# A fused linear-attention and FP4 feed-forward kernel: SyncE's queue reordered, four cast buffers, attention read from four banks at once

## The reference, cut to what matters

```
xn  = layernorm(x)
# branch s: linear attention, then an MLP
a   = rmsnorm(xn);  q, k, v = a @ qkv_w.T          # 16 heads of 64
q, k = exp(-0.5*q*q), exp(-0.5*k*k)                # phi
kv  = k^T v per head, over the whole sequence of 2048 rows (16 tiles)
out = (q @ kv) / (q . sum(k) + 1e-6);  x1 = xn + gamma*(out @ proj_w.T + b)
s   = x1 + gamma*(gelu(rmsnorm(x1) @ conv1_w.T + b1) @ conv2_w.T + b2)
# branch g: feed-forward whose weights and inputs go through blockwise FP4
fq(z): per block of 16: scale = max|z|/6; round z/scale to the FP4 grid; times scale
h   = silu(fq(xn) @ fq(w_gate).T) * (fq(xn) @ fq(w_up).T)
g   = silu(fq(h) @ fq(w_down).T)
out = x + s*g
```

## Time and profile before

| | |
|---|---|
| three runs | 1999.74, 2073.59 and 1997.06 us; median 1999.74 |
| the profiled execution | 1997.77 us; spans of the cores 1979.4 to 1996.2 us |
| the core shown (core 1) | span 1996.2 us, mean granted TensorE clock 0.977 |
| stretch 50 to 484.6 us (stages 2 to 5) | 434.6 us, PE busy 363.1 |
| stretch 484.6 to 1020 us (stage 6) | 535.4 us, PE busy 516.4 |
| stretch 1020 us to the end (stage 7) | 976.2 us, PE busy 962.4 |

### The profile page before, as it was taken

One profiled execution on the slowest core, in us unless ns is written; L12 is line 12 of the kernel. 1 busy time (PEld: TensorE's weight loads), 2 busy tenths in 40 slices (PEclk: granted clock), 3 DMA queues, 4 the chain that ended last, 5 costly groups with the idle time before them and its releaser, 6 DMA issues.

```text
span 1996.2 us, 27757 instructions; the slowest of 8 cores (1979.4 to 1996.2 us)
## 1 busy us (share of the span) xinstructions
PE 1875.5 (94%) x9142; PEld 879.4 (44%) x9142; DVE 1636.2 (82%) x2019; ACT 785.3 (39%) x991; POOL 395.5 (20%) x356
## 2 busy tenths in 40 slices
PE   6988697878999999999999999999999999999997
PEld 3434343333444444444444444444444444444443
DVE  4788878867688688797734999999999999999986
ACT  4676576664433433544521222222222222222221
POOL 3245545534423422422500000000000000000000
PEclk9999898989999999999999999999999999999998
DMA  9788778884455465465599433444334333433322
GB/s 301 199 238 233 226 210 212 229 225 127 115 159 161 109 174 161 101 189 149 127 197 191 126 103 88 95 102 103 94 86 105 103 93 86 105 99 92 88 83 66
DMA packets 367262, 287.07 MB, mean 144 GB/s; under 512 B 299024, under 2 KB 308240, under 8 KB 366096
## 3 DMA queue, kind: packets, MB, share of 16 engines
q1 hardware_dynamic: 367120, 285.29, 55.3%
HBM read 153.63 MB, written 59.24 MB: 107 GB/s over the span
## 4 chain that ended last, share of the span: by engine, by line
PE 71%; DVE 8%; issue 7%; DMA 6%; ACT 3%; POOL 3%; SPq 2%; DVEq 0%; ACTq 0%; POOLq 0%
PE PS L1081 30%; PE PS L1126 15%; PE PS L900 10%; PE PS L883 8%; PE PS L840 5%; DMA xf<-w_gate 2%; DMA wst<-c1T 2%; PE PS L646 1%; DVE q_am L222 1%; DVE atz L817 1%; DVE ob L256 1%; PE PS L588 1%; DVE xf L231 1%; DMA xf<-w_up 1%; DMA phi_h<-pq 1%
## 5 line engine op out<-in xcount | busy, mean ns | idle before, releaser
L240 ACT ACTIVATE gam<-xf 128x1024 bf16<-128x1024 f32 (+1 forms) x196 | 198.1, 1011 | 505.1 <-DVE xf L231 494.5
L1081 PE MATMUL PS<-wg,xqT 128*128 128x512 bf16 (+1 forms) x1536 | 319.9, 361 | 1.7 <-DVE so L910 1.7
L1081 PE MATMUL PS<-wu,xqT 128*128 128x512 bf16 (+1 forms) x1536 | 319.9, 361 | 0.0
L222 DVE TENSOR_REDUCE q_am<-xf 128x64 f32<-128x1024 f32 (+1 forms) x196 | 227.6, 1161 | 74.5 <-DMA xf<-w_up 29.5
L250 DVE SCALAR_TENSOR_TENSOR xf<-gam,xf 128x1024 f32<-128x1024 bf16 (+1 forms) x196 | 233.9, 1193 | 30.0 <-ACT gam L240 29.7
L256 DVE SCALAR_TENSOR_TENSOR ob<-gam,q_sc 128x1024 bf16<-128x1024 bf16 (+1 forms) x196 | 243.0, 1240 | 3.3 <-DVE gam L253 2.8
L231 DVE SCALAR_TENSOR_TENSOR xf<-xf,q_rc 128x1024 f32<-128x1024 f32 (+1 forms) x196 | 238.0, 1214 | 1.9
L253 DVE SCALAR_TENSOR_TENSOR gam<-gam,xf 128x1024 bf16<-128x1024 bf16 (+1 forms) x196 | 235.6, 1202 | 2.1
L883 PE MATMUL PS<-xn2T,c1T_s 128*128 128x512 bf16 x1024 | 234.8, 384 | 2.4 <-DVE kvbd L566 2.4
L1126 PE MATMUL PS<-wdA,hqT 128*128 128x512 bf16 x1024 | 227.8, 380 | 0.4 <-DMA hqT<-ob 0.4
L900 PE MATMUL PS<-c2T_s,hdd 128*128 128x512 bf16 x1024 | 222.3, 379 | 0.0
(11 more groups left out here) (90 smaller groups left out, 1852.8 us busy)
## 6 DMA issues: line engine op xcount, KB each, us to landing
xx<-x SPq DMA_DIRECT2D x32, 512.0 KB, 4.5
xf<-x SPq DMA_DIRECT2D x32, 512.0 KB, 4.2
xr<-x SPq DMA_DIRECT2D x32, 512.0 KB, 4.6
out<-xr SPq DMA_DIRECT2D x31, 512.0 KB, 3.9
xa<-x SPq DMA_DIRECT2D x30, 512.0 KB, 6.0
stg<-qkvT SPq DMA_DIRECT2D x24, 512.0 KB, 13.2
xf<-w_gate SPq DMA_DIRECT2D x22, 512.0 KB, 6.3
xf<-w_up SPq DMA_DIRECT2D x22, 512.0 KB, 5.9
```

The lines of the kernel that those rows point to most:

```text
L222: S.add("v", lambda v: v.tensor_reduce(am, blk(y), AX, op.max, apply_absolute_value=True), waits=[src_ev, opt("q_nq%d" % (k - 3))], ev="q_ ...
L240: S.add("sc", lambda s: s.activation(gam[k % 2][:, 0:W], xf[k % 3][:, 0:W], AF.Abs, scale=BIG), waits=["q_y%d" % k, opt("q_out%d" % (k - 2 ...
L1081: S.add("pe", lambda pe, wts=wts, bi=bi, j=j, b0=b0, ic=ic: pe.matmul(bank(b0 + j, GB[bi][1]), xqT[t % 3][:, ic, :], wts[bi][:, ic, :], st ...
```

## The change

- **SP's order.** The phi(q) stores, the `xn1T` transposes and the `xa` loads that are asked for during one k, v or q group are put into SP's list at the head of the next (`later`, `held`). The store of a finished quantisation task goes behind the next task's load (`unsent`, `send`). Cast loads are asked for after the third group of a tile and not the second.
- **Cast buffers.** `wst` has four buffers for the first 28 pieces and two for the last 12; up to four are loaded ahead.
- **phi(q) buffers.** The last eight q groups have seven buffers (`pqx` and `pq`). `turn(31)` moves from the end of tile 27 behind the second of the 13 q groups.
- **Zeroing.** `zero_acc(1)` moves from tile 16 to the end of tile 17's groups, one tile later.
- **Attention.** From tile 4 on it lies in banks 0 to 3, two pairs of heads in each, and one DVE instruction each makes the denominators and `atz` instead of three. conv1 takes banks 4 to 7, conv2 banks 0 to 3.
- **xn2.** The ACT instruction that writes it is put one group later than the one that takes the squares (`proj_xn2`).

```diff
             [WK + 63552, WK + 64576, WK + 73792])]
-        wst = [at("wst%d" % i, [P, D], F32, WK + 65600 + 4096 * i) for i in range(2)]
+        wst = [at("wst%d" % i, [P, D], F32, o) for i, o in enumerate(
+            [WK + 65600, WK + 69696, W3 + 24576, W3 + 28672])]
+        pqx = [at("pqx%d" % i, [P, 512], BF16, WK + 24576 + 1024 * i) for i in range(4)]
...
                 if n == 1:
+                    send()
...
+        unsent = []
+        def send():
+            while unsent:
+                unsent.pop(0)()
...
-            def post(k):
+            def store(k):
...
                 S.ev[tk["done"]] = S.ev["q_st%d" % k]
+            def post(k):
+                unsent.append(lambda: store(k))
...
                 prev = cur
+            send()
...
                   waits=["mrs%d" % t, "x%d" % t, opt("xn1T%d" % (t - 2))], ev="xn1_%d" % t)
-            S.add("sy", lambda s: s.dma_start_transpose(out=xn1T[:, c, :, :], in_=xn1_of(t)[:]),
-                  waits=["xn1_%d" % t, opt("kv%d_3" % (t - 8)), opt("q%d_7" % (t // 4 - 2))],
-                  inc="XT%d" % (t % 4), ev="xn1T%d" % t)
+            later.append(lambda: S.add(
+                "sy", lambda s: s.dma_start_transpose(out=xn1T[:, c, :, :], in_=xn1_of(t)[:]),
+                waits=["xn1_%d" % t, opt("kv%d_3" % (t - 8)), opt("q%d_7" % (t // 4 - 2))],
+                inc="XT%d" % (t % 4), ev="xn1T%d" % t))
...
+        NW4 = 28
+        def wbuf(n):
+            return n % 4 if n < NW4 else n % 2
...
+            before = [m for m in range(n) if wbuf(m) == b]
...
-            S.add("sy", lambda s: s.dma_start(out=wst[n % 2][:],
+            S.add("sy", lambda s: s.dma_start(out=wst[b][:],
...
-                  waits=[opt("wc%d" % (n - 2))], inc="WS%d" % (n % 2), ev="wl%d" % n)
+                  waits=["wc%d" % before[-1] if before else "kvm3"], inc="WS%d" % b,
+                  ev="wl%d" % n)
...
                 dst = projT[:, ic, :] if kind == "p" else c2T[:, ic, :]
-                S.add("gp", lambda p: p.tensor_tensor(dst, wst[n % 2][:], gm[:], op.mult),
-                      waits=["wl%d" % n, "gm", "kvm3"], ev="wc%d" % n)
+                w = ["wc%d" % (NW4 - 1), "wc%d" % (NW4 - 2)] if kind == "2" and ic >= 12 else []
+                S.add("gp", lambda p: p.tensor_tensor(dst, wst[b][:], gm[:], op.mult),
+                      waits=["wl%d" % n, "gm", "kvm3"] + w, ev="wc%d" % n)
...
         nbank = [0]
+        later = []
+        def held():
+            for fn in [later.pop(0) for _ in range(len(later))]:
+                fn()
...
             b = t % 2
+            held()
...
         def q_group(s, qc):
+            held()
...
             bi, bk = take_bank()
-            pb = pq[n % 3]
+            pb, sem = pq[n % 3], "PH%d" % (n % 3)
+            before = n - 3
+            if n >= 56:
+                i = (n - 56) % 7
+                pb, sem = (pqx + [pq[2], pq[0], pq[1]])[i], "PX%d" % i
+                before = n - 7 if n == 63 or i > 3 else 0
...
             S.add("sc", lambda sc: sc.activation(pb[:], sq[:], AF.Exp, scale=-0.5),
-                  waits=["qr%d" % n, opt("ps%d" % (n - 3))], ev="qe%d" % n)
+                  waits=["qr%d" % n, opt("ps%d" % before) if before > 0 else "xn1_31" if n >= 56
+                         else opt("ps0") if n == 3 else None], ev="qe%d" % n)
...
-            S.add("sy", lambda sc: sc.dma_start(out=g["phi_h"][s, :, qc, :], in_=pb[:]),
-                  waits=["qe%d" % n], inc="PH%d" % (n % 3), ev="ps%d" % n)
+            later.append(lambda: S.add(
+                "sy", lambda sc: sc.dma_start(out=g["phi_h"][s, :, qc, :], in_=pb[:]),
+                waits=["qe%d" % n], inc=sem, ev="ps%d" % n))
...
                       (26, 2): [(turn, 29), (load_x, 31)], (26, 3): [(stats, 30)],
-                      (27, 1): [(turn, 30)], (27, 2): [(stats, 31)], (27, 3): [(turn, 31)]})
+                      (27, 1): [(turn, 30)], (27, 2): [(stats, 31)]})
...
         nw = 0
-        nl = 2
+        nl = 4
...
                     pump(PA[2])
-                if gi == 1 and t > 4:
-                    while nl < min(nw + 2, len(wjobs)):
+                if gi == (2 if nl < NW4 else 1) and t > 4:
+                    while nl < min(nw + (4 if nl < NW4 else 2), len(wjobs)):
...
                 for step, u in AHEAD.get((t, gi), []):
-                    step(u)
+                    if step is load_x:
+                        later.append(lambda u=u: load_x(u))
+                    else:
+                        step(u)
+            if t == 17:
+                zero_acc(1)
+            if t > 4:
+                kv_mm(t - 1)
...
-                kv_mm(t - 1)
...
-                zero_acc(1)
-            elif t > 4:
-                kv_mm(t - 1)
...
-                load_w(0)
-                load_w(1)
+                for n in range(4):
+                    load_w(n)
...
-        XB = [3, 4, 5, 2]
-        YB = [(0, 1), (6, 7)]
+        XB = [4, 5, 6, 7]
+        YB = [(0, 1), (2, 3)]
...
             S.add("sy", lambda y: y.dma_start(out=phq[:], in_=g["phi_h"][s]),
-                  waits=["ps%d" % (8 * s + 7), "ps%d" % (8 * s + 6), "ps%d" % (8 * s + 5), "q6_7",
-                         opt("at%d" % (4 * s - 1))],
+                  waits=["ps%d" % n for n in range(8 * s, 8 * s + 8)] +
+                        ["q6_7", opt("at%d" % (4 * s - 1))],
...
-        AB = [0, 1, 6]
...
-        yfree = ["kvbd1_5", "atz3"]
+        yfree = ["kvbd1_5", "kvbd1_5"]
+        def at_pos(t, p_):
+            if t < 4:
+                return 512 * AB0[p_ // 3] + 130 * (p_ % 3)
+            return 512 * (p_ // 2) + 130 * (p_ % 2)
...
         def attn(t):
...
-                o = 512 * ab[p_ // 3] + 130 * (p_ % 3)
+                o = at_pos(t, p_)
...
                 if p_ == 0:
-                    w += [opt("atz%d" % (t - 1))] + (yfree if s else [bfree[5], bfree[6], bfree[7]])
+                    w += [opt("atz%d" % (t - 1))]
+                    w += yfree if s else [bfree[5], bfree[6], bfree[7]]
+                    w += [bfree[3]] if t == 4 else []
...
             j, b, s = t % 4, t % 2, t // 4
-            views = []
-            for i, n in enumerate((6, 6, 4)):
-                o = 512 * (AB if s else AB0)[i]
-                v3 = PS[:, o:o + 65 * n].rearrange("p (h c) -> p h c", c=65)
-                views.append((6 * i, n, v3))
-            for h0, n, v3 in views:
-                S.add("v", lambda v, h0=h0, n=n, v3=v3: v.tensor_scalar(
-                    den[b][:, h0:h0 + n].rearrange("p h -> p h ()"), v3[:, :, 64:65], 1e-6, None,
-                    op.add), waits=["at%d" % t, opt("zz%d" % (t - 2))], ev="den%d_%d" % (t, h0))
+            if s:
+                views = [(0, 4, 4, PS[:, 0:2048].rearrange("p (a x) -> p a x", a=4)[
+                    :, :, 0:260].rearrange("p a (h c) -> p a h c", c=65))]
+            else:
+                views = []
+                for i, n in enumerate((6, 6, 4)):
+                    o = 512 * AB0[i]
+                    views.append((6 * i, 1, n, PS[:, o:o + 65 * n].rearrange(
+                        "p (a h c) -> p a h c", a=1, c=65)))
+            for h0, na, nh, v4 in views:
+                S.add("v", lambda v, h0=h0, na=na, nh=nh, v4=v4: v.tensor_scalar(
+                    den[b][:, h0:h0 + na * nh].rearrange("p (a h) -> p a h ()", a=na),
+                    v4[:, :, :, 64:65], 1e-6, None, op.add),
+                    waits=["at%d" % t, opt("zz%d" % (t - 2))], ev="den%d" % t)
...
-                  waits=["den%d_12" % t, opt("atz%d" % (t - 2))], ev="zz%d" % t)
-            for h0, n, v3 in views:
-                S.add("v", lambda v, h0=h0, n=n, v3=v3: v.tensor_tensor(
-                    atz[b][:, 64 * h0:64 * (h0 + n)].rearrange("p (h e) -> p h e", e=64),
-                    v3[:, :, 0:64],
-                    zz[b][:, h0:h0 + n].rearrange("p h -> p h ()").broadcast_to([P, n, 64]),
-                    op.mult),
-                    waits=["zz%d" % t, opt("atT%d" % (t - 2)), "xn1_31"],
-                    ev="atz%d" % t if h0 == 12 else None)
+                  waits=["den%d" % t, opt("atz%d" % (t - 2))], ev="zz%d" % t)
+            for h0, na, nh, v4 in views:
+                S.add("v", lambda v, h0=h0, na=na, nh=nh, v4=v4: v.tensor_tensor(
+                    atz[b][:, 64 * h0:64 * (h0 + na * nh)].rearrange(
+                        "p (a h e) -> p a h e", a=na, e=64),
+                    v4[:, :, :, 0:64],
+                    zz[b][:, h0:h0 + na * nh].rearrange("p (a h) -> p a h ()", a=na)
+                    .broadcast_to([P, na, nh, 64]), op.mult),
+                    waits=["zz%d" % t, opt("atT%d" % (t - 2))] +
+                          ["ps%d" % n for n in (56, 57, 58, 59, 63)], ev="atz%d" % t)
...
         def proj(t):
-            n, (b0, b1) = take_y() if t >= 4 else (1, YB[1])
+            n, (b0, b1) = take_y() if t >= 4 else (1, (6, 7))
+            free = yfree[n] if t >= 4 else "x2_%d" % (t - 1) if t else "atz3"
...
```

(27 more changed lines are left out.)

15 lines of the change are left out of this document (8 added, 7 removed).

## The result

Four executions of the changed kernel took 1967.13 to 1970.69 us, median 1967.70. The ratio to the kernel before is 0.9849, 95% interval [0.9826, 0.9873]: 1.5% faster, some 30 us. (Two of the four executions of the kernel before that count here had a die at a lower clock, 2073.59 and 2125.99 us; the ratio leaves them out.) I had predicted 1954 us, in a range of 1926 to 1992.

What follows compares the result with a forecast made beforehand. It took the stretch from 50 to 484.6 us as bound by who waits for whom, not by an engine. From 1997.8 us, -40 there and -5 in attention gave 1952.8, or 1954.7 against the median; predicted 1954 us, range 1926 to 1992.

Steps and rivals of the forecast that it cites:

- The clearing wait: Before conv1, PE waits for DVE's `kvbd` copies before clearing banks; zeroing a tile later hides it: -9.3 us.
- a new wait for the transpose of tile 31: Among the last q groups, PE waits 3.4 us anew; an old wait of 3.87 goes: 0 in sum.
- The attention part: After 484.6 us, 0.56 us less DVE work a tile shortens PE's waits for `atz`: -5 us, bounds 0 and -12.
- PE's path: Stretch from 50 to 484.6 us: PE's removed gaps and higher clock shorten its path by 47 us.
- DVE's path: Same first stretch: DVE needs 391 us, 43 less, from work 342.5, remaining idle 36 and collisions 13.
- The cast's gaps: First stretch: seven PE gaps behind ACT's waits for `c1T` go with four cast buffers: -12.8 us.
- new collisions with POOL: First stretch: POOL casts that met an idle DVE may now meet a working one, adding 13 us.
- The clock: First stretch: PE runs slower after long gaps; five gaps over 2.3 us go, 1.8 each: -9 us.
- (a): Rival: DVE stays the bound in the first stretch, loads land later; DVE gives 15 us, attention 5: 1978 us, chance 0.22.
- (b): Rival: the change doesn't do what it says; only the zeroing goes, 5 us on the path: 1993 us, chance 0.08.
- (c): Rival: more gained in first stretch; last `c1T` waits shorten too and clock stays up: 1930 us, chance 0.10.
- (d): Rival: slower; later `xn1T` transposes make PE wait 3.9 us in each of 22 tiles, +86: 2040 us, chance 0.05.

Runs made afterwards that it cites:

- mended kernel: Changed kernel with tile 31's transpose one q group earlier, last q group in group 60's buffer, four cast buffers through piece 31: 1959.67 us, ratio 0.9777.
- attention run: Kernel before with only attention over four banks, one `atz`, conv1 and projection in other banks, `xn2` one group later: 1987.67 us, ratio 0.9922.
- after, thin tasks: Changed kernel with the planner's front allowances for DVE tasks cut from 1600, 700, 1500 to 1400, 600, 1300 ns: 1970.08 us, ratio 0.9826.
- before, thin tasks: Kernel before, two cast buffers, with front allowances for DVE tasks cut from 1600, 700, 1500 to 1400, 600, 1300 ns: 1994.93 us, ratio 0.9946.
- after, less DVE work: Changed kernel with two of five long DVE passes of 36 tasks over 64 of 1024 columns, leaving out computation: 1944.92 us, ratio 0.9704.
- mended, thin tasks, more in conv: Mended kernel with front allowances 1400, 600, 1300 ns and the allowance behind each conv2 half raised from 2850 to 3250 ns: 1958.87 us, ratio 0.9782.
- mended, thinner still: Mended kernel with allowances for DVE tasks of 1200, 500, 1100 ns in the front and 800, 700, 3450 in the conv rounds: 1980.20 us, ratio 0.9901.

## Why the prediction was wrong

**What held.** The clearing wait of 9.28 us is gone; ACT's wait for `c1T` fell to 11.7 us, where I said 14; one `atz` takes 1225 ns; the last stage did not move; a new wait for the transpose of tile 31 came, 7.56 us and not 3. The attention part was 6.3 us in the conv rounds where I had 5, and the two gaps that it takes from the end of the front, 6.6 us in my sum, gave 6.2.

**The step that failed** is the sum of PE's path, 12.8 + 9.3 + 13.4 + 2.3 + 9 = 47 us, and the 43 us of DVE's path beside it. I summed PE's gaps as if each were worth its length. For the gaps in tiles 4 to 27 the runs show that most of their length was not on the path. The cast's gaps were put at 12.8 us; removing them gave 4.6 alone and no gain that can be seen in the changed kernel (the last pieces' wait of 8.98 us, mended, gave 3). The clearing's 9.3 gave 3.2. In the mended kernel, cores whose TensorE runs at 0.81 for 150 us lose nothing. What sets this part is DVE's line of quantisation steps, fixed in place among the other instructions: 68 us of its busy time removed take 28.5 us off, and four or five of its tasks moved elsewhere, of 7.4 us each by the means of their seven instructions, take 15 to 19 off, in both kernels. The moved tasks also took some 5 us of ACT's and 9 to 13 us of POOL's busy time out of the front, so how much of the 15 to 19 us is DVE's alone is not shown.

Behind tile 27 it is otherwise: there gaps of PE did pay (6.2 of 6.6 us above, and some 3.5 us of the late transpose of tile 31), though not all: the 4.52 us at `atz` gave nothing. The 6.8 us of the phi(q) buffers have no run of their own.

**DVE's own sum** went wrong in its idle time. I let all of the 56.3 us for `xf` go and none come. 21 went. The loads take 0.5 us longer each, DVE waits 8.1 us for ACT's `gam` where it had waited 2.5, and 4 us for the phi(q) stores at `atz`. Idle time of DVE fell from 92.1 to 80.2 us on the two cores shown, and from 89.9 to 73.3 by the median over the cores; I had 36. Its work stayed the same (340 and 339 us by that median), so that the 18 us of the front are nearly all idle time of DVE. The 13 us of new collisions with POOL did not come: DVE's three long passes took 1453, 1312 and 1343 ns where they had taken 1275, 1352 and 1514, a sum of 4108 against 4141. On the sentence on the shared port pair in the Trainium skill ("SBUF — State Buffer") I had rested that the 13 us were a floor. No run here tests it: I had worked them out for 56 us of closed gaps, and 12 closed on the core shown.

**The clock.** Core 3 shows 0.93 in the front as core 1 did. From 50 to 450 us the eight cores show 0.93 to 0.94 before and 0.94 to 0.96 after; behind the clearing, from 225 to 250 us, they showed 0.75 to 0.81 and now show 0.89 to 1.00. An estimate from these: 0.01 to 0.02 of the 345 us that PE is busy, 3 to 7 us of its work, and not 9. As the slowed cores of the mended kernel show, time of TensorE in this part was not on the path. Also, the gaps over 2.3 us that go by my own list are six (4.62, 2.35, 9.28, 8.65, 4.20, 2.43) and not five.

**The new wait of `atz` for the last phi(q) stores**, put at 0, was 4.52 us of PE, and the pieces after 28, for which I counted nothing, cost one wait of 8.98 us: the kind of wait of which I had said that its growth would prove me wrong, 7.31 us of ACT before and 9.23 now. With the late transpose, 7.56 us where I had 3.4, these are three waits that the change itself made or left; mending them gave 6 to 8 us.

**What I left out:** the task stores behind the next load give 6 us in the conv rounds too. I had looked for the effect of SP's queue in the front alone. Which loads it had held back in the conv rounds is not shown.

In sum: front -18 where I had -40, conv rounds -13 where I had -5. Of the rivals (a), "DVE stays the bound", had the front nearly right, 15 us, and in part for its reason: of the 56.3 us of waiting 35.0 stayed, and the loads take longer to land. It was off in the conv rounds, by the 6 us of the task stores. (b) and (c), 25 us above the measured median and 38 below it, did not come. (d) didn't occur: in the front SP's order gave 7 us, and transposes land in 5.6 us.

The parts alone sum to 0.23 + 0.16 + 0.79 + 0.78 = 1.96%, the whole gave 1.51. The intervals of the two, some 0.35% and 0.24% to either side, overlap, so that a difference is not shown. The buffers `pqx` and the new place of `turn(31)` are in none of the parts.

## What to carry to other kernels

An engine's gaps may be summed only after asking whether that engine sets the pace, and in which part of the stage; thinning the work of the suspected engine by a few per cent in one stage, or finding a core whose clock happened to be lower, tests that in one run. Where cores at a lower clock turn up in some executions only, they have to be set apart before two kernels are compared. When a wait is taken away and the same engine's wait for another one rises by nearly as much, the first wait had covered the second. Where a list order is written out by hand, read the change's last pieces too (the last buffer, the last tile, the point where four buffers become two): three such ends were worth about a quarter as much as the whole change.

## What the runs showed of the hardware

In many executions one or more pairs of neighbouring cores (0 and 1, 2 and 3, 4 and 5, or 6 and 7) have a granted TensorE clock of 0.81 from 75 to 225 us, in each 25 us of it, and a higher one after that in most of them (0.93 or more from 225 to 350 us in the mended kernel); with one pair of the attention run it began only between 100 and 200 us; the engine had been working since the start, and its clock was 1.00 in the first 50 us. The pair's mean clock over the execution is then 0.012 to 0.015 lower, by which the pairs are counted here. It occurred with every kernel but the changed one, and each of the four pairs had it: 51 of 164 pairs of the kernel before, 5 of 16 of the mended one, none of the 16 of the changed one, but 8 of 20 of the changed one with two cast buffers. What it costs depends on who sets the front, by the median span of cores with and without it (of the kernel before, the 13 executions beside the first parts):

| kernel | without | with |
|---|---|---|
| before | 1993.8 | 1992.1 |
| after, three waits mended | 1953.0 | 1952.8 |
| after, thin tasks | 1954.6 | 1963.4 |
| before, thin tasks | 1973.1 | 1985.0 |
| after, less DVE work | 1928.2 | 1942.0 |
| mended, thin tasks, more in conv | 1941.8 | 1954.3 |
| mended, thinner still | 1947.4 | 1975.0 |

The less the front waits for DVE, the more a pair at 0.81 costs, up to 28 us in these rows, and since the metric is the slowest core, one such pair sets it. So the 18 us that the thin mixture gains on undisturbed cores over the changed kernel (1959.6 to 1941.8) shrink to 9 in the measured median. What brings it about stays open.
